# A transformer-like layer on one core: new order at the front of each round, work moved from ScalarE and VectorE to VectorE and GpSimd, and a GpSimd power put ahead of the last decay operand

## The reference

```python
h = _layernorm(x, ln1_w, ln1_b); x1 = x + _mamba2(h, ...)
s = x1 + gelu(_layernorm(x1, ln2_w, ln2_b) @ w1.T + b1) @ w2.T + b2
x2 = x + attention(_rms(x, n1_w));  xf = _rms(x2, n2_w)
f = x2 + sum(wts[e] * expert_e(xf));  out = x + s * silu(f)
```

## Time and profile before

| what | value |
|---|---|
| median of 3 runs | 860.65 us (860.46 to 865.01) |
| profiled execution, its own time | 861.28 us |
| its span | 859.5 us |
| TensorE busy | 784.9 us (91%) |
| VectorE busy | 618.1 us (72%) |
| ScalarE busy | 498.5 us (58%) |
| GpSimd busy | 320.8 us (37%) |
| granted TensorE clock, mean | 0.993 |

### The profile page before, as it was taken

The page is one execution under the profiler, slowest core; times in us unless marked ns, Lnnn a source line. Parts: engine busy times, 40 slices in busy tenths (PEclk is TensorE's granted clock), DMA queues, the critical chain, the costliest instruction groups (busy, mean ns, idle before and its releaser), DMA issues. The chain is left out here.

```text
span 859.5 us, 18101 instructions
## 1 busy us (share of the span) xinstructions
PE 784.9 (91%) x5472; PEld 482.5 (56%) x5472; DVE 618.1 (72%) x1469; ACT 498.5 (58%) x928; POOL 320.8 (37%) x600
## 2 busy tenths in 40 slices
PE   2779999998999989998999989999899998999897
PEld 1455564755557465665647555475556656475545
DVE  2786479785887768786697858877587876967534
ACT  2435784476753776457844767537764568447552
POOL 5424543053512717036340535227170362505400
PEclk9999999999999999999999999999999999999999
DMA  4000000000000000000000000000000000000000
GB/s 166 2 8 17 12 0 1 9 16 25 0 8 12 14 12 0 8 14 25 0 0 8 14 24 0 6 13 14 12 0 8 13 25 0 0 8 14 24 2 13
DMA packets 15145, 11.73 MB, mean 14 GB/s; under 512 B 1040, under 2 KB 13968, under 8 KB 14992
## 3 DMA queue, kind: packets, MB, share of 16 engines
q1 hardware_dynamic: 15120, 11.43, 4.4%
HBM read 7.76 MB, written 2.10 MB: 11 GB/s over the span
## 5 line engine op out<-in xcount | busy, mean ns | idle before, releaser
L1102 ACT ACTIVATE sb_pr<-S 128x768 f32<-128x768 f32 (+1 forms) x192 | 161.2, 878 | 135.0 <-PE S L445 134.9
L1198 DVE TENSOR_REDUCE sb_mx<-S 128x2 f32<-128x256 f32 (+3 forms) x256 | 198.0, 818 | 32.8 <-PE S L445 31.6
L1722 POOL TENSOR_SCALAR_AFFINE_SELECT sb_pr<-sb_pr 128x256 f32<-128x256 f32 (+1 forms) x192 | 98.8, 520 | 301.7 <-ACT sb_pr L1102 301.0
L445 PE MATMUL R<-sb_pr,sb_va 128*32 128x512 f32 (+3 forms) x1024 | 89.7, 445 | 6.3 <-POOL sb_pr L1722 6.3
L445 PE MATMUL R<-sb_W,sb_pr 128*128 128x96 f32 (+1 forms) x512 | 69.5, 276 | 0.0
L445 PE MATMUL R<-sb_xfT,sb_W 128*128 128x512 f32 x144 | 69.2, 602 | 0.0
L445 PE MATMUL S<-sb_kT,sb_qT 32*128 32x256 f32 (+3 forms) x512 | 56.0, 383 | 14.2 <-DVE sb_mx L1198 10.7
L445 PEld LDWEIGHTS R<-sb_W,sb_pr 128*128 128x128 f32 x512 | 63.5, 192 | 3.8 <-issue 3.5
L445 PEld LDWEIGHTS S<-sb_kT,sb_qT 32*128 32x128 f32 x512 | 27.4, 182 | 67.0 <-DVE sb_mx L1198 59.2
L1432 DVE SCALAR_TENSOR_TENSOR sb_x<-R,sb_wts,sb_x 128x96 f32<-128x96 f32 x128 | 40.6, 317 | 22.8 <-PE R L445 19.4
L445 PE MATMUL S<-sb_qT,sb_kT 32*128 32x256 f32 (+3 forms) x512 | 56.1, 383 | 0.5 <-ACT sb_pr L1102 0.5
(11 more groups left out here) (217 smaller groups left out, 1708.7 us busy)
## 6 DMA issues: line engine op xcount, KB each, us to landing
sb_xin<-x SPq DMA_DIRECT2D x9, 256.0 KB, 2.8
sb_W<-weights SPq DMA_DIRECT2D x1, 2290.0 KB, 11.6
sb_qT<-sb_mT SPq DMA_DIRECT2D x128, 4.0 KB
sb_xres<-x SPq DMA_DIRECT2D x8, 256.0 KB, 2.8
out<-sb_xres SPq DMA_DIRECT2D x7, 256.0 KB, 2.3
sb_cT<-sb_xact SPq DMA_DIRECT2D x8, 128.0 KB, 2.3
sb_W<-weights SPq DMA_DIRECT2D x1, 514.0 KB, 5.6
sb_cst<-consts SPq DMA_DIRECT2D x1, 328.0 KB, 3.1
```

What stands on the lines that cost most here:

```text
L445: return pe.matmul(o, lhsT, rhs, start=start, stop=stop, skip_group_check=True)
L1102: act.activation(pr[:, e % 4, :, 0:n], S[pair_of_exp(e)][:, :, 0:n], ACT.Exp).then_inc(p_sb, 1)
L1198: o = dve.tensor_reduce(mx[:, n // P - 1, g, heads[0]:heads[1] + 1], found[:, :, at_col:at_col + n], AX.X, ALU.max, negate=True)
L1722: pool.affine_select(out=keep, in_=keep, compare_op=ALU.is_ge, fill=0.0, base=0, pattern=pattern, channel_multiplier=-1)\
```

## The change

Four things. (1) TensorE's front gets a new order: the projection of q, k, v for tile 0 goes to the end of stage A of the round before (ahead of the last turn of y), tile 1 after the turn of oT and ahead of `op`, tiles 2 and 3 after the turn of ao; `project_x(0)` comes after `wo`, `z` later, the turn of xf ahead of the first group of tokqk turns and the gate products between the groups 3 and 4. (2) ScalarE no longer copies v; VectorE does, in two pairs. (3) x1n and xf move from VectorE to GpSimd. (4) In stage A of GpSimd, step 2 of the next norm goes ahead of the decay operand of chunk 3. ScalarE's two `cv` operations go behind the four qT, and its squares of x2 are split in two pairs; VectorE's gate operations go between the second and the third kT; xfT's evacuation goes behind z and x1T.

```diff
 # tensor
+            def project_qkv(r, t):
+                mm(bank(t)[:, 0:3 * D], xbT[:, t * P:(t + 1) * P], w("qkv")).then_inc(qkv_ps, 1)
...
                     i.then_inc(ot3_ps, 1)
+                if head:
+                    project_qkv(r, 1)
+                if tail:
...
-                if head:
-                    pe.wait_ge(xbT_sb, at(xbT_sb, r, 0))
-                    pe.wait_ge(p_sb, at(p_sb, r, 0))
-                    for t in range(T):
-                        mm(bank(t)[:, 0:3 * D], xbT[:, t * P:(t + 1) * P], w("qkv")).then_inc(qkv_ps, 1)
...
                 if head:
-                    project_x(r, 0)
+                    project_qkv(r, 2)
+                    project_qkv(r, 3)
...
                     for n in range(2 * G):
+                        if tail and n == 0:
+                            turn_second_norm(r)
+                        if tail and n == T:
+                            gate(r)
...
                 weigh_values(r, G * UNITS - 2)
+                pe.wait_ge(xbT_sb, at(xbT_sb, r, 1))
+                pe.wait_ge(p_sb, at(p_sb, r, G * UNITS))
+                project_qkv(r, 0)
                 turn_y(r, T - 1)
 # scalar
                 if head:
-                    evac_qkv(r)
+                    evac_qkv(r, (0, 1))
                 if tail:
                     act.wait_ge(aoT_ps, at(aoT_ps, r, 1))
                     act.activation(aoT[:], R[0][:, :], ACT.Copy).then_inc(aoT_sb, 1)
                 if head:
+                    evac_qkv(r, (2, 3))
...
-                            if tail:
-                                gate_exp(r)
-                elif tail:
+                if head:
+                    for n in range(2):
...
+                        act.activation(cv[:, n], xc[:, n, TAPS - 1:TAPS - 1 + L], ACT.Identity,
...
+                if tail:
                     gate_exp(r)
 # vector
+            def evac_values(r, ts_):
...
+                for t in ts_:
+                    dve.wait_ge(qk_sb, at(qk_sb, r, t + 1))
+                    ts(va[:, t, :, 0:HD], bank(t)[:, 2 * D:3 * D].rearrange("p (h d) -> p h d", h=AH),
+                       ratio[:, t:t + 1], None, ALU.mult).then_inc(qkv_sb, 1)
...
                 if tail:
                     values(r, 3, ot3_ps, ao3_sb)
+                if head:
+                    evac_values(r, (0, 1))
...
+                if head:
+                    evac_values(r, (2, 3))
 # gpsimd
+            def first_norm(r):
+                pool.wait_ge(r2_sb, at(r2_sb, r, 2))
...
+                for t in range(T):
+                    i = ts(x1n[:, t, :], x1[:, t, :], mv2[:, t, 0:1], r2[:, 1, t:t + 1],
+                           ALU.subtract, ALU.mult)
+                i.then_inc(x1n_sb, 1)
+
             def stage_b(r, tail, head):
+                if tail:
+                    first_norm(r)
                 if head:
                     pool.wait_ge(sq_sb, at(sq_sb, r, 1))
...
                        ALU.mult).then_inc(qw_sb, 1)
+                    if tail:
+                        second_norm(r)
                     pool.wait_ge(lo_sb, at(lo_sb, r, 1))
...
+            def second_norm(r):
+                pool.wait_ge(r3_sb, at(r3_sb, r, 2))
...
+                for t in range(T):
+                    i = ts(xf[:, t, :], x2[:, t, :], r3[:, 1, t:t + 1], 0.0, ALU.mult, ALU.add)
+                i.then_inc(xf_sb, 1)
...
+                    if e == NORM_AT[2]:
+                        first_norms(r, 2)
                     if u == 5 and g < T - 1:
                         decays(r, g + 1, tail)
-                    if e in NORM_AT:
+                    if e in NORM_AT[0:2]:
                         first_norms(r, NORM_AT.index(e))
```

More of the change, by code:

```diff
@@ L745, in stage_b @@
                     project_x(r, 2)
+                    project_z(r, 1)
                     project_z(r, 2)
-                if tail:
[L748 to L752, removed]
-                    project_z(r, 3)
[L754 to L759, removed]
+                    project_z(r, 3)
+                if tail and not head:
+                    turn_second_norm(r)
+                    dense(bank(0)[:, 0:256], 1)
+                    gate(r)
                 if head:
                     for n in range(2 * G):
+                        if tail and n == 0:
+                            turn_second_norm(r)
+                        if tail and n == T:
+                            gate(r)
                         if n == 0:
@@ L917, in _, with evac_qkv @@
         def _(act):
[L918 to L922, removed]
+            def evac_qkv(r, ts):
+                if 0 in ts:
+                    act.wait_ge(rn_sb, at(rn_sb, r, 0))
+                    act.wait_ge(lo_sb, at(lo_sb, r, 0))
+                    act.wait_ge(pv_ps, at(pv_ps, r, 0))
+                for t in ts:
                     act.wait_ge(qkv_ps, at(qkv_ps, r, t + 1))
                     act.activation(qk[:, t].rearrange("p a h d -> p (a h d)"), bank(t)[:, 0:2 * D], ACT.Copy,
[L925 to L928, removed]
+                                   scale=ratio[:, t:t + 1]).then_inc(qk_sb, 1)
             def evac_maxima(r, pair, o):
@@ L1015, in stage_b @@
                 if tail:
-                    act.wait_ge(x2_sb, at(x2_sb, r, 2))
-                    act.wait_ge(yss_sb, at(yss_sb, r, 0))
-                    for t in range(T):
+                    for t in range(2, T):
                         i = act.activation(junk[:, t // 2, t % 2 * D:t % 2 * D + D], x2[:, t, :], ACT.Square,
@@ L1040, in stage_b @@
                     evac_z(r, 3)
[L1042 to L1048, removed]
+                if tail:
+                    act.wait_ge(x1T_ps, at(x1T_ps, r, 1))
+                    act.activation(x1T[:], R[1][:, :], ACT.Identity, bias=vec[:, V_LN2B:V_LN2B + 1],
+                                   scale=vec[:, V_LN2W:V_LN2W + 1]).then_inc(x1T_sb, 1)
+                    evac_xf(r)
+                if head:
                     act.wait_ge(e_ps, at(e_ps, r, 0))
@@ L1350, in stage_b @@
                 if tail:
[L1351 to L1356, removed]
+                    pass
                 if head:
+                    dve.wait_ge(sq_sb, at(sq_sb, r, 1))
+                    dve.tensor_reduce(rqk[:, 0], sq[:].rearrange("p t a h d -> p (t a h) d"), AX.X,
+                                      ALU.add).then_inc(ssqk_sb, 1)
                     dve.wait_ge(rqk_sb, at(rqk_sb, r, 2))
@@ L1385, in stage_b @@
                        ALU.subtract).then_inc(lo_sb, 1)
-                for _ in gate:
-                    pass
+                gate = gate_logits(r) if tail else iter(())
+                if not head:
+                    for _ in gate:
+                        pass
                 if head:
@@ L1392, in stage_b @@
                         dve.tensor_copy(kT[:, g, :], bank((2 * g + 1) % 4)).then_inc(kT_sb, 1)
+                        if g == 1:
+                            for _ in gate:
+                                pass
                     dve.wait_ge(xc_sb, at(xc_sb, r, 3))
@@ L1640, in stage_b @@
                     tt(sp[:, 1], sp[:, 1], sp[:, 0], ALU.subtract).then_inc(spa_sb, 1)
+                if tail and not head:
+                    second_norm(r)
                 if tail:
                     pool.wait_ge(x1n_sb, at(x1n_sb, r, 1))
-                    pool.sem_inc(pool_passed, 1)
                     tt(x1[:], x1[:], row[:, R_B2:R_B2 + D].unsqueeze(1).broadcast_to([P, T, D]),
@@ L1663, in stage_b @@
                     time_steps(r)
+            def second_norm(r):
+                pool.wait_ge(r3_sb, at(r3_sb, r, 2))
+                pool.sem_inc(pool_passed, 1)
+                pool.wait_ge(xfT_ps, at(xfT_ps, r, 0))
+                pool.sem_inc(pool_passed, 1)
+                pool.wait_ge(x2_sb, at(x2_sb, r, 2))
+                pool.sem_inc(pool_passed, 1)
+                for t in range(T):
+                    i = ts(xf[:, t, :], x2[:, t, :], r3[:, 1, t:t + 1], 0.0, ALU.mult, ALU.add)
+                i.then_inc(xf_sb, 1)
             def time_steps(r):
```

81 lines of the change are left out of this document (48 added, 33 removed).

## The result

| | before | after |
|---|---|---|
| median | 862.83 us (4 runs, 860.46 to 865.05) | 912.64 us (4 runs, 911.04 to 914.46) |
| ratio, 95% interval | | 1.0578 (1.0535 to 1.0622) |
| span of the profiled execution | 859.5 us | 909.3 us |
| TensorE / GpSimd busy | 784.9 / 320.8 us | 806.1 / 376.9 us |
| granted TensorE clock, mean | 0.993 | 0.957 |

The change costs 49.8 us; 6.4 was forecast, in a range that ended at 873.5. The sign was right, the size far off.

A forecast was written before the change was run, and what follows sets the result against it. TensorE, busy 91% of the span, was taken as the bound, with waits in two places the change touches. Swap +4.0, front +2.1 and last round +0.3 made 6.4 us, some 867.0 us; own range 863.5 to 871, eight in ten 857.5 to 873.5.

The forecast's parts named there:

- the swap: Stage A, power ahead of chunk 3's decay operand: 0.25 to 0.68 us lost a round, taken as 0.5, eight times +4.0 us.
- I take 0.31: Front, GpSimd: time in us for one x1n tile, between 0.18 and 0.34; 1.25 us for four.
- The meeting of xf: Front: xf on GpSimd runs beside VectorE's norm and casts; 0.49 us, taken once, puts `lo_sb` at 322.2.
- the late end: Front: all 1.25 us of xf fall between VectorE's operations, `lo_sb` at 322.95; the sum would be 13 us instead of 6.4.
- 2.68 us: Stage A, GpSimd: length of step 2 of the norm, from 296.14 to the mask at 298.82.
- it all arrives: Stage A: TensorE runs without a wait from `segments(3)` to the last turn of y, so the swap's whole loss counts.
- The gate's operations of VectorE: Front: six operations between kT's, where VectorE waits for gate and turns anyway; nothing, at worst 0.2 us.
- the gate in the open: Front, TensorE: gate products between the fourth and fifth group of turns, 0.45 us more a round after the wait for qT goes.
- 4.7 said: Front, TensorE: from first turn of tokqk to last end 3.72 + 1.0 = 4.7 us, 4.27 before.
- no wait for the gelus: ScalarE: gelus begin 1.5 to 2 us later behind the `cv` pair, at no cost; otherwise up to 1.5 us a round.
- the port is shut: Rival, chance 0.13: GpSimd's xf and VectorE's operations take turns, `rs` waits for xres; +13.1 us, 873.8.
- a gain of 0.1 us a round: Front: with x1n and xf on GpSimd and one meeting, `lo_sb` comes at 322.2, 0.1 us earlier.

The follow-up runs named there:

- e7: The changed kernel with x1n's tiles 1 to 3 on GpSimd given other pairs of operations, tile 0 keeping subtract and mult; 898.79 us in one run.
- e11: The changed kernel with x1n alone back on VectorE, xf still on GpSimd; 891.72 us, 1.0333 against the kernel before.
- e4: The kernel before with only the power put ahead of the decay operand of chunk 3; 884.51 us, 1.0263.
- e6: The swap-only kernel with five unread 128x256 products on TensorE ahead of its wait for the decay operand; 874.05 us, 1.0124 against the kernel before.
- e10: The changed kernel with unread products filling TensorE's waits, five ahead of the decay operand, seven ahead of x1n; 906.13 us, 1.0486 against the kernel before.
- e3: The changed kernel with swap undone and both norms back on VectorE, leaving the new order and the values' copies; 872.27 us, 1.0096 against the kernel before.
- e8: The kernel before with step 2 of the norm behind unit 21's mask, xa's turns and copies at the end of stage A; 858.00 us, 0.9932.
- e12: The kernel before with late xa turns and late cv pair, the power behind unit 19 and its three products behind unit 21; 847.73 us, 0.9835.
- e2: The changed kernel with x1n and xf back on VectorE, the swap kept; 890.11 us, 1.0319 against the kernel before.

## Why the prediction was wrong

Two steps failed about equally, the price of x1n in the front and the size of the swap.

**The front: "I take 0.31" for a tile of x1n.** It came from 0.70 us for a 128x512 of the same kind, bounded by 0.18 and 0.34; it measured 0.79. Three things were missing. The upper bound was summed wrongly: with half of 0.70 fixed, a quarter of the columns costs 0.35 + 0.09 = 0.44, not 0.34, and xf, the same operation as that row, takes 0.37 alone. x1n has a second operand per partition: 0.44 to 0.46 with the cheap pairs (e7). And the row is no subtraction, which brings it to 0.79. The working around it held: the second part of the first root ends 8.14 us behind the last turn of y after, 8.17 by the sketch; then 3.13 instead of 1.25 us for x1n puts the norm of q and k at 13.09 us instead of 10.96. That is 2.1 of the 2.3 us by which the first turn is late. (The 0.35 us for marker steps came from no row; from the root's end to x1n it was 0.48 us.)

**The meeting of xf** was taken "once", 0.49 us. GpSimd was held up in most tiles, xf took 4.35 us, but VectorE's two casts took 1.29 us as before: VectorE was not the one that paid. The rule in the Trainium skill, SBUF — State Buffer, Who interferes with whom, which I had set beside the late end, agrees in that GpSimd is shut out for whole operations of VectorE (a tile of 1.33 us beside a norm of 1.32, two of 1.35 beside pairs of casts and differences). That xf would then be what TensorE waits for was in no case of mine; with x1n back it is worth 1.6 us, which the intervals do not tell from nothing (e11).

**The swap** was sized at 0.25 to 0.68 us a round and cost 2.8 on average (e4), 2.2 in the new order (17.8 us in eight). The order of events was right, the masks' wait gone, a longer one for `rs` in its place. Its "2.68 us" for step 2, read where its small products met nothing, was 3.53 beside xres; so `segments(3)` started 2.1 us later than before (2.91 us behind the turn of y, 0.78 before) instead of 1.1 to 1.5, and "it all arrives" left out that the work behind it could run slower.

**What no term held** is the clock. The profile before shows 1.00 in the stretch behind the front, and I summed waits at their length. Behind most waits of 2.5 us TensorE's work ran at about half speed; filling them gave 10.5 of 22 us back (e6). In the front the same drop was mostly hidden by the wait for xf, and showed when the first wait was filled (e10).

**The gate's operations of VectorE** ("nothing, at worst 0.2") took 2.55 us instead of 1.1 where GpSimd's convolution ran, and TensorE waited 1.35 us for kT in e3: with it the order cost 9.9 us, where the gate in the open had been given 0.45 a round.

**What held:** the `rs` wait in place of the masks', the first turn of tokqk within 0.1 us without GpSimd's norms (15.44 against 15.53, e3), 4.50 us from the first turn to the last end (4.7 said), tile 0's projection in the idle time ahead of the turn of y, and no wait for the gelus. Of the rivals, "the port is shut" named the right direction, at 13 us of 50. The sign came out right by the swap and the gate; the norms on GpSimd, which lose 18 to 22 us, had been taken as a gain of 0.1 us a round. The range failed because the upper bound for x1n was summed wrongly, and because each other size came from one row that met little and stood at full clock.

## What to carry to other kernels

Before a small operation is moved to another engine, find a row there with the same operation and not only the same shape: one `subtract` made a tile cost 0.80 us instead of 0.45. A new wait of 2 us or more on TensorE has to be priced twice, once with the work behind it at full speed and once at half, since here both occurred behind the same wait; and filling it pays only if the next thing that TensorE waits for is not late itself. A long power in a queue belongs behind the last operand that TensorE waits for, in a gap that the trace shows: put later it made the kernel 0.7% faster (e8), and split, together with the later `cv` pair, 1.65% (e12), where ahead of that operand it made it 2.6% slower (e4).

## What the runs showed of the hardware

- GpSimd's tensor_scalar of 128x128 float32 with two operands per partition: 0.79 to 0.80 us with subtract and mult, 0.44 to 0.46 with add and mult, mult and mult, or mult and add (e7); with one operand per partition and mult and add 0.37 (xf in the last round). Why the subtraction is dearer stays open.
- Behind a wait of 2.47 us on TensorE the granted clock stood at 0.50 to 0.56 for some 7 us (e4, r = 0), behind one of 3.40 at 0.61 over the next 4.3 us (after). The wait just ahead does not settle it: behind a wait of 2.47 us the clock stayed at 1.00 in two of seven rounds of e2, and in the four us from a turn of x1n that had waited 2.19 us it was 1.00 at 217.3 and 0.64 at 627.3 in the same run (e3). Nor is a short wait safe: the profile before keeps 1.00 behind the front, but has 0.57 from 802 to 806 and 0.58 from 120 to 124, with no wait of TensorE over 0.93 us near either. What decides was not found.
- In two meetings of GpSimd and VectorE the operation that started second waited. A tile of xf that started at 227.7, behind VectorE's norm (227.49), took 1.33 us instead of 0.37, and the norm 1.32 instead of 1.22; VectorE's 128x16 operation that started at 235.79, behind GpSimd's 128x512 product (235.73), took 1.24 us instead of 0.17, and the product its usual 1.27. GpSimd's 128x4 product at 308.96 does not fit: it started 0.13 us ahead of xres and still took 0.90 us instead of 0.20.
- e10's runs spread over 9 us, and the mean granted clock goes with them: 0.985 in the run of 899.67 us, 0.968 in that of 908.92. It is so in other kernels too (e3: 0.994 at 868.37, 0.982 at 874.32; before: 0.993 at 860.90, 0.982 at 867.55).
